# A linear-attention and FFN block on one core: sixteen spans written out instead of a loop over twelve of them

## What is computed

```python
xn = layernorm(x)
q, k, v = xn @ Wq, xn @ Wk, silu(xn @ Wv)          # 16 heads of 32
q, k = q / |q| * 32 ** -0.5, k / |k|
beta = sigmoid(xn @ Wb)
# per head, over the tokens in order:
#   delta = (v_t - S^T k_t) * beta_t;  S += k_t delta^T;  o_t = S^T q_t
o = o * rsqrt(mean(o * o) + 1e-5) * o_norm_weight
ffn = (silu(xn @ q8(gate_w) * gate_scale) * (xn @ q8(up_w) * up_scale)) @ q8(down_w) * down_scale
return x + o @ Wo + ffn
```

## Time and profile before

| what | value |
|---|---|
| median of 3 runs | 2532.01 us (2530.65 to 2535.6) |
| the profiled execution's own time | 2530.2 us |
| its span, first to last instruction | 2528.5 us |
| granted TensorE clock, mean over the span | 0.995 |
| PE busy | 2342.3 us, 93% |
| DVE busy | 1865.5 us, 74% |
| ACT, POOL busy | 853.9 us, 315.1 us |

### The profile page before, as it was taken

The page is one execution under the profiler, slowest core; times in us unless marked ns, Lnnn a source line. Parts: engine busy times, 40 slices in busy tenths (PEclk is TensorE's granted clock), DMA queues, the critical chain, the costliest instruction groups (busy, mean ns, idle before and its releaser), DMA issues.

```text
span 2528.5 us, 93373 instructions
## 1 busy us (share of the span) xinstructions
PE 2342.3 (93%) x40992; PEld 1270.7 (50%) x40992; DVE 1865.5 (74%) x3211; ACT 853.9 (34%) x2070; POOL 315.1 (12%) x544
## 2 busy tenths in 40 slices
PE   0099999999999999999999999999999999999996
PEld 0045545455555545555554555545454554555553
DVE  7977686967768696776858677686866769586775
ACT  2135252423425242342524334252422425233241
POOL 4510201001020100102010010201001010100100
PEclk9999999999999999999999999999999999999998
DMA  5100000000000000000000000000000000000000
GB/s 175 63 10 11 3 18 20 18 20 18 19 3 18 20 18 20 19 19 3 19 21 18 20 19 19 3 18 20 18 20 20 19 3 18 20 18 20 16 22 19
DMA packets 27204, 54.68 MB, mean 22 GB/s; under 512 B 5152, under 2 KB 5152, under 8 KB 26784
## 3 DMA queue, kind: packets, MB, share of 16 engines
q1 hardware_dynamic: 26784, 48.55, 5.7%
HBM read 31.76 MB, written 16.78 MB: 19 GB/s over the span
## 4 chain that ended last, share of the span: by engine, by line
PE 88%; DVE 7%; issue 3%; DMA 0%; POOL 0%; ACT 0%; DVEq 0%; SPq 0%
PE T L339 22%; PE D L416 21%; PE D L485 14%; PE D L426 11%; PE D L427 11%; PE D L355 7%; PE D L344 1%; DVE outer_v L1102 1%; DVE kq L257 1%; DVE fuse L1095 1%; DVE at L1109 1%; DVE kpv L1199 1%; DVE at L853 0%; DVE f_lo L852 0%; DVE w_lo L894 0%
## 5 line engine op out<-in xcount | busy, mean ns | idle before, releaser
L426 PE MATMUL D<-xt_hi,wgu 128*128 128x512 f16 x1536 | 582.3, 379 | 0.3
L427 PE MATMUL D<-xt_lo,wgu 128*128 128x512 f16 x1536 | 582.1, 379 | 0.0
L416 PE MATMUL D<-xt_hi,w_hi 128*128 128x512 f16 x832 | 318.4, 383 | 6.7 <-issue 6.7
L416 PE MATMUL D<-xt_lo,w_hi 128*128 128x512 f16 x832 | 317.9, 382 | 0.0
L416 PE MATMUL D<-xt_hi,w_lo 128*128 128x512 f16 x768 | 293.6, 382 | 0.0
L485 PE MATMUL D<-wd,f_hi 128*128 128x512 bf16 x768 | 293.1, 382 | 0.0
L485 PE MATMUL D<-wd,f_lo 128*128 128x512 bf16 x768 | 292.4, 381 | 0.0
L1109 DVE TENSOR_TENSOR at<-at,outer_v 128x62 f32<-128x62 f32 (+15 forms) x496 | 263.3, 531 | 15.5
L1102 DVE TENSOR_TENSOR outer_v<-mt,at 128x62 f32<-128x62 f32 (+15 forms) x496 | 259.8, 524 | 9.4
L426 PEld LDWEIGHTS D<-xt_hi,wgu 128*128 128x128 f16 x1536 | 150.3, 98 | 184.7 <-DVE fuse L1095 5.3
L427 PEld LDWEIGHTS D<-xt_lo,wgu 128*128 128x128 f16 x1536 | 150.3, 98 | 179.6
(11 more groups left out here) (158 smaller groups left out, 3259.9 us busy)
## 6 DMA issues: line engine op xcount, KB each, us to landing
xs<-_attn_hidden_states_dram SPq DMA_DIRECT2D x34, 512.0 KB, 3.5
out_dram<-xs SPq DMA_DIRECT2D x32, 512.0 KB, 3.0
f_hi<-in_L_ffn_down_w_dram SPq DMA_DIRECT2D x4, 768.0 KB, 4.6
kq<-in_L_ffn_gate_w_dram SPq DMA_DIRECT2D x3, 768.0 KB, 4.4
f_hi<-in_L_ffn_up_w_dram SPq DMA_DIRECT2D x2, 768.0 KB, 5.8
kq<-in_L_ffn_up_w_dram SPq DMA_DIRECT2D x2, 768.0 KB, 6.2
qt<-in_L_attn_Wq_dram SPq DMA_DIRECT2D x1, 1024.0 KB, 8.1
kpv<-in_L_attn_Wk_dram SPq DMA_DIRECT2D x1, 1024.0 KB, 10.4
```

Source lines behind the costliest of these rows:

```text
L416: last = nc.tensor.matmul(D[bank][:, :], w[:, k, cols], xp[:, k, :], start=n == 0, stop=n == len(products) - 1)
L426: nc.tensor.matmul(D[bank][:, :], wgu[:, k, c:c + P], xt_hi[:, k, :], start=k == 0, stop=False)
L427: last = nc.tensor.matmul(D[bank][:, :], wgu[:, k, c:c + P], xt_lo[:, k, :], start=False, stop=k == KT_ - 1)
```

## The change

`TURNS` becomes 16. `some_spans(0)` then writes out all sixteen spans, and the four `Fori` loops of PE, ACT, POOL and DVE are taken out. SP's loop passes `turns=2` itself and stays as it is. No computing instruction is added, removed or put in another place.

```diff
@@ -20,7 +20,7 @@
-TURNS = 4
+TURNS = 16
@@ -550,8 +550,6 @@
             some_spans(0)
-            with pe.Fori(1, SPANS // TURNS) as it:
-                some_spans(it)
@@ -692,8 +690,6 @@
             some_spans(0, first=True)
-            with act.Fori(1, SPANS // TURNS) as it:
-                some_spans(it)
@@ -806,8 +802,6 @@
             some_spans(0)
-            with pool.Fori(1, SPANS // TURNS) as it:
-                some_spans(it)
@@ -1220,8 +1214,6 @@
             some_spans(0, first=True)
-            with dve.Fori(1, SPANS // TURNS) as it:
-                some_spans(it)
```

## The result

The changed kernel takes 2518.0 us (median of 6 runs, 2514.6 to 2520.6) against 2531.4 us of the kernel before in the same measurement (2526.9 to 2535.6). The ratio is 0.9944, with a 95% interval of 0.9927 to 0.9961: 13.4 us less, where 11 were forecast. The median lies 3 us from the predicted 2521 and inside the range. The profiled execution has a span of 2517.7 us, 10.8 less than before.

What follows compares the result with a forecast made beforehand. PE was taken to bound the kernel. 2530.2 - 7.0 (jumps) - 3.4 (clock) - 2.9 (register work) + 2.0 (packet borders) = 2518.9 us; with 1.8 us from profiled execution to median, 2521 us, range 2513 to 2529.

Steps and rivals of the forecast that it cites:

- What bounds the kernel: Whole kernel: only PE's stream counts, busy 93% of the span; savings on ACT, DVE and POOL are worth nothing by themselves.
- Part 1, the jumps: Two taken loop branches, before spans 8 and 12: PE's pauses of about 3.5 us each vanish, worth 7.0 us.
- The rival that the pause is a meeting of the engines: At the jumps: engines meet at the span's end and the 3.8 us pause stays, so no change, 2531 us; chance 3%.
- Part 2, the clock: Behind both jumps, spans 8 and 12: PE's half-clock stretches after the pause vanish, 1.7 us each, worth 3.4 us.
- without the pause there is nothing before it that differs: Spans 8 and 12: with the pause gone, what precedes them is like spans 1 to 6, which kept clock 1.00.
- granted clock of 1.00 in every span: Sign in the profile after: PE's clock full in every span, low only in the tail behind the last span.
- The clock's rival: Half-clock stretches belong to the passage of time and come back elsewhere: +3.4 us, 2524 us; chance 6%.
- Part 3, register work on PE: Spans 4 to 15: removing register operations saves 0.2 us a span, plus 0.5 for loop entry and set-up; worth 2.9 us.
- Part 4, the packet borders: Small matmul bursts: instruction packet boundaries shift and PE's stalls there change by +2.0 us, between -4 and +7.
- 35 us and called 46 wrong: Sign in PE's waits: small-burst stalls near 35 us in place of 33.0; 46 us or more would refute the forecast.
- the places come back after seven spans: Packet boundaries shift by 37 instructions a span, so spans 7 and 14 stall where span 0 does.
- the rival that all spans might stall like span 15: Spans 4 to 15 each stall 3.8 us in bursts: +21.2 in place of +2, 2540 us, slower; chance of slower 4%.

Runs made afterwards that it cites:

- e3: Kernel before with only PE's sixteen spans written out; ACT, POOL and DVE keep the loop over bodies of four: 2512.4 us, ratio to before 0.9961.
- e4: Kernel before with ACT, POOL and DVE written out while PE keeps its loop: 2526.6 us against 2522.0, ratio 1.0020.
- e1: Kernel before with eight spans written out and a loop body of eight run once, so no taken branch: 2511.2 us, ratio to before 0.9954.
- e9: The kernel before, unaltered, run once more for a second trace: ratio to before 0.9994.
- e10: Changed kernel with PE made to wait for a DVE sum at the head of spans 8 and 12: 2526.6 us, ratio to before 1.0002.
- e5: The changed kernel, unaltered, run once more: 2511.7 us against 2526.7, ratio 0.9944.
- e7: Changed kernel with 64 tiny matmuls in front of the first span, moving all packet borders by half a packet: 2509.9 us, ratio to before 0.9940.
- e8: Changed kernel with each tile stored and loaded by itself, so half of a transfer goes earlier: 2512.6 us, ratio to before 0.9944.
- e2: Kernel before with a loop body of two spans run seven times, six taken branches: 2531.9 us, ratio to before 1.0038.
- e11: The kernel before with a loop body of two spans, measured and traced a second time: 2531.4 us against 2526.8, ratio 1.0025.
- e6: Changed kernel with the second sequence's loads and stores cut to 8 of 128 partitions: 2504.6 us, ratio to before 0.9927.

## Why the prediction was right, point by point

**What bounds the kernel** was right: only PE's stream counts. e3 brings the gain without the other engines, e4 nothing without PE.

**Part 1, the jumps, 7.0 us:** right. The trace has 7.0 us less at the borders, and e1 wins the gain by taking out nothing but the taken branches and the register work of four spans. In other traces with the same stream on PE (e9, e4) the two pauses together are 6.5 us. The rival that the pause is a meeting of the engines falls with e1, e3 and e4.

**Part 2, the clock, 3.4 us:** cause and size were right, one step of the reasoning was not. e10 shows that a pause alone does it. But the step "without the pause there is nothing before it that differs" failed: stalls of 2 us in the bursts also lower the clock, at times, and so the granted clock of 1.00 in every span, which was forecast, was not seen. In the traces with PE in the loop of four (before, e9, e4) a half-clock stretch follows five of the six jumps, and 0, 1 and 1 stand elsewhere. In those without a taken jump (after, e5, e3, e1, e7, e8) there are 2, 0, 1, 0, 1 and 0, so what stands elsewhere is about as frequent with the jumps as without them. The change takes away those at the jumps: dense matmuls are late by 7.0, 5.4 and 7.6 us in the first three traces and by 3.4, 2.2 and 3.4 in after, e5 and e3, 3.7 fewer in the mean, with a scatter of 2. The clock's rival, that the lost stretches come back elsewhere, is not borne out.

**Part 3, register work on PE, 2.9 us:** no run shows this term. What remains of sixteen spans without pauses, stalls and late dense matmuls is 2308.3, 2309.9 and 2310.6 us with register work in twelve spans (before, e9, e4), 2310.1, 2308.5 and 2308.4 without (after, e5, e3), 2308.4 with it in eight spans (e1), and less still with it in fourteen (e2, e11). The first two means are 0.6 us apart, with 2 us between traces of one kind. All that can be pointed at is 0.3 us at the loop's entry. The term is thus mis-sized: by these means it is well under 2.9, and how near to nothing the scatter doesn't let one say. The step that failed was to read the 0.4 to 1.1 us by which pairs of loop spans are longer than spans 1 and 2 as a price of 0.2 a span. The stalls of single spans differ by up to 2.9 us from one trace of a program to the next (e5), which I had not measured.

**Part 4, the packet borders, +2.0 us with -4 to +7:** the sum is right within its scatter, the model behind it only half. Mean of three traces each by my count: 46.5 us in the loop (51.5, 41.6, 46.4), 45.4 written out (50.4, 38.2, 47.7), so -1 where I took +2. In the view of waits, in which the forecast gave 35 us and called 46 wrong, the changed kernel has 32.4. The stalls do stand at the borders and move with them (e7), and the places come back after seven spans as forecast. But that their lengths come back too was wrong: span 7, which should repeat span 0's 3.7, had 1.3, and had 0.85 and 4.1 in e5 and e3 with the same stream. How long a stall is depends on more than its place. One part of it is seen in the trace and fits e6: a data transfer in front of the packet. The other is a guess that was not tested: how far PE's queue still reaches when the border comes, which depends on when DVE let the burst begin.

**The sum.** The size came out partly by luck: the 2.9 us of part 3 are not there, and 3 us of stalls that were expected to come did not. By the means of the three traces before, e9 and e4 against after, e5 and e3, the pauses are 6.7 us less, the late dense matmuls 3.7, the stalls 1.1 and the rest 0.6, together 12 us against the 11.3 that I summed. The measured 13.4 and 15.0 us (e5) and the 9.6 of e3 lie on both sides; the interval of 0.9927 to 0.9961 is 10 to 18 us. Single traces are worth little here, with 14 us between two of the same program.

**Slower:** the rival that all spans might stall like span 15 never came near. Nowhere did sixteen spans add up to more than 52 us.

## What to carry to other kernels

Count the taken branches on the engine that bounds, price each by the distance between the last instruction in front of it and the first behind it, and add the slow clock where that engine is PE; the register operations in this loop's body, where dense matmuls are mostly queued ahead of them, had no price that could be told from the scatter. A kernel that has a part written out and a part in a loop shows the price of its loop in its own trace, but take two traces before reading differences of 0.3% between spans. If a large loop body is wanted for code size, a single round of it (e1) wins as much as no loop.

## What the runs showed of the hardware

- A taken branch on PE at the end of a body of 4 spans stopped it for 2.9 to 3.4 us (before, e9, e4), with a body of 2 spans for 2.1 to 2.6 us (e2, e11); an untaken one took 83 ns. In all eighteen cases PE went on 1.5 to 1.7 us after the packet fetched at the jump had landed.
- Half-clock stretches of 3.41 us followed both pauses of 4.7 us, five of six of 2.9 to 3.4 us (before, e9, e4; one of these stretches lasted 6.83 us), seven of twelve of 2.1 to 2.6 us (e2, e11), and ten of the nineteen stalls of 1.7 to 2.2 us within bursts in all traces, but no shorter stall. So a pause of about 2 us is enough at times.
- A packet of 16 KB with PE's next instructions takes about 1 us to fetch in a stall and 1.0 to 2.2 us at a jump, but started as late as the end of a 0.5 MB data transfer (829.87 us in the changed kernel), and PE went on 2.4 us after its start.
- Executions of one program in one measurement differed by up to 20 us of 2530 (e2, 2518.7 to 2539.0). Between the two traces of the changed kernel it was 14 us, and 12 of them were stalls of PE within its bursts, at the borders of its instruction packets.
